# Row statistics of the first block-sparse layer made in attention's block, its bias and centroid operations apart from them, the weights' high parts on VectorE

## The reference

```python
x = x + attn_a(layernorm(x), w_attn, w_proj, adapter_wte, gating)   # 32 heads, rotary, adapter prefix
x = x + ffn(layernorm(x), weight, bias, centroids, assignments)     # first block-sparse layer
x = x + attn_b(layernorm(x), in_proj_w, conv_w, ..., out_w)         # state-space mixer, 128 heads
x = x + ffn(layernorm(x), weight, bias, centroids, assignments)     # the same layer again
...
def layernorm(x):
    m = mean(x, axis=-1); v = var(x, axis=-1)
    return (x - m) / sqrt(v + 1e-5)

def ffn(x, weight, bias, centroids, assignments):       # x: 1024 x 512, weight 512 x 512, 64 centroids
    dots = softmax(x @ centroids.T / 0.1, axis=-1)
    hits = dots > 0.01
    query_sel, cluster_sel = any(hits, axis=1), any(hits, axis=0)
    row_sel = cluster_sel[assignments]
    dense = x @ weight.T + bias
    return where(query_sel[:, None] & row_sel[None, :], dense, 0)
```

## Time and profile before

| | us |
|---|---|
| median of 3 runs | 1915.48 (1914.93 to 1915.66) |
| the profiled execution | 1914.4 |
| its span | 1912.7 |
| TensorE matmuls busy | 1817.4 (95%) |
| TensorE weight loads | 1454.2 (76%) |
| GpSimd | 1434.0 (75%) |
| VectorE | 1340.3 (70%) |
| ScalarE | 1163.2 (61%) |

### The profile page before, as it was taken

The page is one execution under the profiler, slowest core; times in us unless marked ns, Lnnn a source line. Parts: engine busy times, 40 slices in busy tenths (PEclk is TensorE's granted clock), DMA queues, the critical chain, the costliest instruction groups (busy, mean ns, idle before and its releaser), DMA issues.

```text
span 1912.7 us, 29241 instructions
## 1 busy us (share of the span) xinstructions
PE 1817.4 (95%) x10780; PEld 1454.2 (76%) x10780; DVE 1340.3 (70%) x1703; ACT 1163.2 (61%) x2105; POOL 1434.0 (75%) x1429
## 2 busy tenths in 40 slices
PE   6998897878999999999999999999999999999977
PEld 4776675667887888888888888888888888888866
DVE  5664564666767777687668767876777687678656
ACT  3222432358676777676676757766777577676752
POOL 4312333638997999799969978997899799979972
PEclk9997997989999999999999999999999999999999
DMA  3000001013222222222222222222322223213201
GB/s 111 1 2 23 2 1 59 12 55 104 90 83 83 78 94 100 67 90 88 89 78 78 94 72 86 94 91 70 96 78 94 72 89 99 95 62 115 72 23 44
DMA packets 107025, 135.54 MB, mean 71 GB/s; under 512 B 9026, under 2 KB 74690, under 8 KB 106884
## 3 DMA queue, kind: packets, MB, share of 16 engines
q1 hardware_dynamic: 105924, 133.63, 21.3%
q10 hardware_dynamic: 960, 0.05, 0.0%
HBM read 131.02 MB, written 2.62 MB: 70 GB/s over the span
## 4 chain that ended last, share of the span: by engine, by line
PE 78%; DVE 2%; POOL 1%; issue 1%; ACT 1%; DVEq 0%; POOLq 0%; ACTq 0%
PE ps L144 20%; PE ps L146 20%; PE ps L145 20%; PE ps L1928 7%; PE ps L1885 3%; PE ps L1929 3%; PE ps L1074 2%; PE ps L1913 1%; PE ps L1946 1%; PE ps L1948 0%; DVE mix_xT L1667 0%; DVE mix_u L1791 0%; PE ps L116 0%; POOL ffn_ln_mv L72 0%; DVE mix_xnT_lo L132 0%
## 5 line engine op out<-in xcount | busy, mean ns | idle before, releaser
L144 PE MATMUL ps<-mix_xnT_hi,mix_w_hi 128*128 128x512 f32 x1152 | 463.1, 402 | 9.5 <-DVE mix_bT L1667 9.5
L146 PE MATMUL ps<-mix_xnT_hi,mix_w_lo 128*128 128x512 f32 x1152 | 455.5, 395 | 0.0
L145 PE MATMUL ps<-mix_xnT_lo,mix_w_hi 128*128 128x512 f32 x1152 | 455.1, 395 | 0.0
L1667 DVE SCALAR_TENSOR_TENSOR mix_xT<-ps,mix_cur,mix_xT 128x510 f32<-128x510 f32 x378 | 279.2, 745 | 144.1 <-ACT mix_xT L1482 135.1
L1393 POOL TENSOR_SCALAR_AFFINE_SELECT mix_spread<-mix_spread 128x256 f32<-128x256 f32 x512 | 305.7, 631 | 0.0
L1687 DVE TENSOR_TENSOR mix_decay<-mix_decay,mix_cb 128x1536 f32<-128x1536 f32 x128 | 293.8, 2333 | 4.9 <-ACT mix_decay L1508 4.7
L1531 ACT ACTIVATE mix_g_hi<-mix_gated 128x512 fp32r<-128x512 f32 x128 | 81.0, 633 | 328.3 <-POOL mix_gated L1370 173.2
L144 PEld LDWEIGHTS ps<-mix_xnT_hi,mix_w_hi 128*128 128x128 f32 x1152 | 217.8, 189 | 58.4 <-issue 11.1
L146 PEld LDWEIGHTS ps<-mix_xnT_hi,mix_w_lo 128*128 128x128 f32 x1152 | 217.4, 189 | 50.9
L145 PEld LDWEIGHTS ps<-mix_xnT_lo,mix_w_hi 128*128 128x128 f32 x1152 | 217.9, 189 | 47.1
L1506 ACT ACTIVATE mix_decay<-mix_spread,mix_cur_ncum 128x256 f32<-128x256 f32 x512 | 253.7, 495 | 0.0
(11 more groups left out here) (262 smaller groups left out, 3327.0 us busy)
## 6 DMA issues: line engine op xcount, KB each, us to landing
mix_spread<-cum_rows SPq DMA_DIRECT2D x128, 512.0 KB, 4.0
mix_w_raw<-in_w_in_stream SPq DMA_DIRECT2D x144, 256.0 KB, 4.2
mix_wo_raw<-in_w_out_T SPq DMA_DIRECT2D x64, 256.0 KB, 3.6
att_w_raw<-in_w_attn_T SPq DMA_DIRECT2D x12, 256.0 KB, 4.1
x<-in_x SPq DMA_DIRECT2D x8, 256.0 KB, 4.4
out_rows<-x SPq DMA_DIRECT2D x8, 256.0 KB, 2.1
att_wp_raw<-in_w_proj_T SPq DMA_DIRECT2D x4, 256.0 KB, 2.6
mix_bT<-in_w_ffn_T SPq DMA_DIRECT2D x2, 512.0 KB, 4.9
```

Of the source, the lines that this page charges most:

```text
L144: pe.matmul(out, lh, rh, start=(k == 0), stop=False)
L145: pe.matmul(out, lh, rl, start=False, stop=False)
L146: last = pe.matmul(out, ll, rh, start=False, stop=(k == tiles - 1))
L1667: dve.scalar_tensor_tensor(out=d[:, :, shift:T], in0=src[:, :, 0:T - shift], scalar=w[:, MK - 1 - shift:MK - shift], in1=d[:, :, shift:T], ...
```

## The change

The statistics' two small tensors (`ffn_stats`, `ffn_mv`) are now allocated once for the whole program. In attention VectorE makes the statistics of row tiles 0 to 6 right after it has added the projection to x (`FFN_DONE` = 7), after a wait for that addition. GpSimd makes the scale and shift of these seven tiles behind its last mask, still in attention's block, on four semaphores of attention's own. In the layer only tile 7 is left: ScalarE waits for "shift" with tile 7 alone. GpSimd's list becomes `make`, the rows of tile 7, `split_bias` parts 0 and 1, `c_low`, `split_bias` part 2, `w_low`, `one_hot`. The centroids' high part moves on ScalarE from behind tile 1 to behind tile 2. The weights' four high parts leave ScalarE and stand on VectorE, behind the low parts of tiles 4, 5, 6 and 7. The last block-sparse layer keeps its order.

```diff
     def normalize_act(act, t):
-        act.wait_ge(ln.s["shift"], t + 1)
+        at_least(act, ln.s["shift"], t + 1 - done)
...
+            for t in range(FFN_DONE):
+                layernorm_rstd(pool, t, sh.ffn_mv, sh.mhalf, ffn_s, 0)
...
                 elif stage == "project":
                     dve.tensor_tensor(x[:, t, :], x[:, t, :], bank(n), ALU.add).then_inc(aux_free, 1)
+                    if t < FFN_DONE:
+                        dve.wait_ge(aux_free, n + 1)
+                        layernorm_stats(nc, dve, x, t, sh.ffn_stats, sh.ffn_mv, ffn_s, 0)
...
+FFN_DONE = NT - 1
...
+    def w_high_dve(dve, k):
+        dve.wait_ge(w_in, 32)
+        dve.tensor_copy(m.w_hi[:, k, :], m.w_raw[k // 2][:, k % 2, :]).then_inc(w_hi_done, 1)
...
             ln.hi_act(act, t)
-            if t == 1 and makes:
+            if t == 2 and makes:
                 act.wait_ge(c_in, 32)
                 act.copy(m.c_hi, m.c_raw).then_inc(c_done, 1)
-            if t >= NT - KT and makes:
-                w_high(act, t - NT + KT)
...
+    def first_rows_dve(dve):
+        for t in range(ln.done, NT):
+            ln.stats_dve(dve, t)
+        for t in range(NT):
+            ln.lo_dve(dve, t)
+            if t >= NT - KT:
+                w_high_dve(dve, t - NT + KT)
...
             f.make(pool)
-            for t in range(4):
+            for t in range(FFN_DONE, NT):
                 fln.rstd_pool(pool, t)
+            for part in range(2):
+                f.split_bias(pool, part)
             f.c_low(pool)
-            for part in range(3):
-                fln.rstd_pool(pool, 4 + part)
-                f.split_bias(pool, part)
-            fln.rstd_pool(pool, 7)
+            f.split_bias(pool, 2)
             for k in range(KT):
                 f.w_low(pool, k)
...
-            f.rows_dve(dve, lambda t: None)
+            f.first_rows_dve(dve)
```

More of the change, by code:

```diff
@@ L78, with build_layernorm @@
     pass
-def build_layernorm(nc, sh, ctx, tag, bank0, n=NT, into=None, banks=2, xn=None):
+def build_layernorm(nc, sh, ctx, tag, bank0, n=NT, into=None, banks=2, xn=None, kept=None, done=0):
     ln = Shared()
     ln.n = n
-    ln.stats = ctx.enter_context(nc.sbuf_tensor(tag + "_stats", [P, NT, 6], F32))
-    ln.mv = ctx.enter_context(nc.sbuf_tensor(tag + "_mv", [P, NT, 2], F32))
+    ln.stats, ln.mv = kept or (ctx.enter_context(nc.sbuf_tensor(tag + "_stats", [P, NT, 6], F32)),
+                               ctx.enter_context(nc.sbuf_tensor(tag + "_mv", [P, NT, 2], F32)))
+    ln.done = done
     ln.xn = xn
@@ L98, in stats_dve @@
     def stats_dve(dve, t):
-        layernorm_stats(nc, dve, sh.x, t, ln.stats, ln.mv, ln.s, 0)
+        layernorm_stats(nc, dve, sh.x, t, ln.stats, ln.mv, ln.s, -done)
     def rstd_pool(pool, t):
-        layernorm_rstd(pool, t, ln.mv, sh.mhalf, ln.s, 0)
+        layernorm_rstd(pool, t, ln.mv, sh.mhalf, ln.s, -done)
     def normalize_act(act, t):
-        act.wait_ge(ln.s["shift"], t + 1)
+        at_least(act, ln.s["shift"], t + 1 - done)
         at_least(act, ln.s["turned"], t - 1)
@@ L599, in build_attention @@
         y_inv, y_ready, y_hi_done = sem("y_inv"), sem("y_ready"), sem("y_hi_done")
+        ffn_s = {k: sem("ffn_" + k) for k in ("stat", "veps", "rstd", "shift")}
         block = ctx.enter_context(nc.Block())
@@ L1095, in layer_parts @@
     f.add_part, f.wait_x, f.rows_act, f.rows_dve, f.find_mask = add_part, wait_x, rows_act, rows_dve, find_mask
+    f.first_rows_dve = first_rows_dve
     f.take_dense, f.cluster_logits, f.turn_logits, f.dense_rows = take_dense, cluster_logits, turn_logits, dense_rows
@@ L1160, in build_mixer @@
         xn = square[:, :].rearrange("p (s c) -> p s c", c=C)
-        fln = build_layernorm(nc, sh, ctx, "ffn1_ln", 6, into=(xnT_hi, xnT_lo), xn=xn)
+        fln = build_layernorm(nc, sh, ctx, "ffn1_ln", 6, into=(xnT_hi, xnT_lo), xn=xn,
+                              kept=(sh.ffn_stats, sh.ffn_mv), done=FFN_DONE)
         chunks = lambda ap: ap.rearrange("p (k c) -> p k c", c=C)
@@ L2090, in build @@
         sh.mhalf = sb("minus_half", [P, 1])
+        sh.ffn_stats, sh.ffn_mv = sb("ffn_stats", [P, NT, 6]), sb("ffn_mv", [P, NT, 2])
         sh.x_arrived = [sh.sem(f"x_arrived{t}") for t in range(NT)]
```

## The result

The change takes 1907.94 us (median of 16 runs, 1901.62 to 1912.56) against 1915.04 us before (16 runs beside them, 1908.59 to 1916.23): ratio 0.9968, 95% interval 0.9959 to 0.9978. The prediction was 1913.5 us with "within 0.2%" at 0.81.

The account below looks back on a forecast made before the run. TensorE was 78% of the chain; the change acts where GpSimd's layer norm delays the cluster logits. 1.9 - 0.9 + 1.0 = 2.0 us earlier gave 1912.4 us, 1913.5 for the median, range 1911.0 to 1915.4.

Parts of the forecast that it names:

- GpSimd stood before the bias: First sparse layer: GpSimd waits 4.4 us for the bias transfer, taken to land at 329.5, holding up the centroids' low part.
- the first half: First 12 matmuls of the cluster logits: start at 333.8 instead of 335.70, 1.9 us earlier, mostly at low clock.
- tile 6 was turned: Transpose of tile 6 behind the logits' first half: 4.8 us after its start instead of 3.9, giving 0.9 back.
- from there to the second half: Tile 6's transpose to the logits' second half: 3.04 us instead of 4.06, gaining 1.0.
- Statistics in attention: Seven tiles' row statistics moved to VectorE in attention: cost on the path 0; 0.9 a tile if cover were gone.
- no weight was late: GpSimd's weight low parts end near 343.9, dense rows ask about 345.5: hidden by 1.5 us.
- A: Bias lands early or clock stays high in the logits' first half: gain 4.1 or 4.0, about 1911.4 us; chance 0.14.
- B: VectorE's copies collide with GpSimd at the shared port: gain only 0.4, time 1915.1 us; chance 0.13.
- C: Statistics lie on attention's path, delaying the yT copy: 3.2 us slower, 1918.7 us; chance 0.06.
- D: Barrier behind attention waits for GpSimd's tile 6, margin 0.5 us: gain 1.0, time 1914.5 us; chance 0.07.
- Nothing behind it has its own appointment: Behind the logits' second half: whatever comes earlier at its entrance stays earlier to the end, so the gain is 2.0 us.
- the sum's last line: Whole kernel: profiled 1914.4 - 2.0 = 1912.4 us, so 1913.5 for the median, from 1915.48 over three runs.

Follow-up runs that it names:

- the two kernels with a shorter first half: Change with centroids first, bias loaded earlier and unread matmuls in the layer (second: also in attention's last steps): 1903.21 us, 0.9960; 1906.20 us, 0.9968.
- the kernel with the new order alone: Kernel before with the change's GpSimd order, centroids' high part behind tile 2 and weight casts on VectorE, statistics still in the layer: 1914.85 us, one execution.
- the third: A further comparison of the unaltered change against the kernel before: ratio 0.9987, difference of means 2.1 us.
- The statistics alone: Change with only the statistics moved, GpSimd's old order kept (centroids first) and high parts back on ScalarE: 1907.53 us, ratio 0.9976 against before.

## Why the prediction failed

**What held.** GpSimd stood before the bias (4.4 us forecast, 4.95 measured, 4.4 to 5.1 in the four other executions). The centroids' low part stood behind it, the first half came 11.62 behind the start (11.38) and at the low clock, tile 6 was turned 4.26 us later (4.8; in the others 4.5 to 4.9), and from there to the second half it took 2.93 (3.04). The cast on VectorE was 0.42 alone (0.49). Statistics in attention cost nothing (1.0002), no weight was late. Each rival was thereby decided in its mechanism. A's does not hold: the bias is a brake, and the clock was low. B's collisions cost about 0.1 in the change, but 0.8 to 1.0 in the two kernels with a shorter first half. C did not occur, by the additions that moved by nothing. Nor did D, as GpSimd's first memset followed attention's end by 1.1 us before and now (322.42 - 321.3, 319.15 - 318.04).

On the landing of a small transfer, the Trainium skill (DMA: Bandwidth & Descriptors, "Queues, rings and completion order") says that completion is not in order of issue over one engine's transfers, but also that each DMA engine takes the descriptors of a ring in order. Here the order of issue decided: issued behind the weights the bias took 4.3 to 5.1 us in the executions of before and of the change, ahead of them 1.84. On the port, the Trainium skill (SBUF — State Buffer, "Who interferes with whom") says that casts from SBUF to SBUF can take the port pair that VectorE shares with GpSimd. The trace agrees: 0.98 and 1.46 us beside GpSimd, 0.42 alone.

**The step that failed** is in the first part: what the change is worth "is how much earlier than 343.65 that second half starts", with "Nothing behind it has its own appointment". TensorE's clock has one. Between the halves of the logits the kernel before left TensorE nearly idle, and in three of the five executions the clock then fell in the second half, which cost 1.6 us there. The sum had this term at nothing. (How far the idle time is the cause is shown in part only: matmuls in it removed the fall in two executions of two, but the kernel with the new order alone had the fall with the change's short wait.) The profile that I had shows an execution in which it did not, and gives 2.4 us for the layer; over five executions each, before has 26.3 us to the dense rows and the change 23.1, so **3.3 us**. The prediction had weighed the clock only in the first half.

**The second step** is the sum's last line. It took one profiled execution and three runs within 0.7 us as the kernel's own time. 16 runs of the same kernel spread over 7.6 us, 102 over 14. A forecast of 2.0 us from 1915.48 was thereby read against a median that lay 2.4 above the mean of all runs. Against that mean, 1913.1, the change's 1908.9 is a gain of 4.2 (2.9 to 5.5): the layer's 3.3 us lie within it, the 2.0 of the forecast do not. The first comparison alone, about 6 us, overstated it, and the third, 0.9987 (0.9970 to 1.0004), would have been called no change.

Together these make up the 5.6 us between the forecast of 1913.5 and the first comparison's 1907.94: 2.4 for the starting value, 1.3 for the layer, 0.9 of gain that nothing here explains, and 0.9 by which these 16 runs lay below the mean of the change's 42.

**Why a shorter layer isn't a shorter kernel to the same amount.** From the first dense row on, the same code took 1564.5 to 1569.3 us in the ten executions. Three stretches differ, each by 2.5 to 2.8 us: from the start of the eighth dense row to the mixer's first exponential of the decay 56.8 to 59.6 us, from there to the main loop's last product with the decay 1416.8 to 1419.3, and from that to the last layer's logits 35.1 to 37.6. The statistics alone gained 2.7 us on the change in the layer, and took 60.3 us for the first of these stretches, where the change mostly took 58.3. Whether the time at which a kernel gets there decides this was not tested; it is a matter of 2 us either way.

**What stays open:** the 0.9 us between 3.3 and 4.2, which is inside the interval. Attention's end: in the eleven profiles with the statistics in attention and nothing else added there it lies at 314.5 on average, in the eight without them at 316.5. Single ones lie from 311.8 to 321.3, so this is no clear difference, and the two executions alike to 0.02 us speak against one. And why the clock falls in before's second half in executions whose attention ends by 319.2 and not where it ends at 321.3, with TensorE as idle ahead of it, or in the kernel with the new order alone, which stands no longer than the change.

## What to carry to other kernels

Before a saving is measured from one profile, ask for a second execution of the same kernel, and see which stretches differ: here attention's end by 9.5 us, and the very layer by 1.6. Where TensorE stands nearly idle ahead of dense work, look in several executions whether its clock falls in that work, and count the slow matmuls as a possible part of the price: here 1.6 us in three executions of five. A collision that one order escapes can come back when something ahead of it gets faster, as the weight cast did (0.42 us, then 1.23 and 1.42). When a queue is reordered, look for the operation that waits for a transfer: what stands behind it inherits the wait (2.6 to 3.3 us here, for one line's place), and issuing that small transfer ahead of the large one cures it too.

## What was not expected of the hardware

- The granted clock of one kernel differs between executions by place: the same 12 matmuls take 2.8 us at 2.4 GHz and 5.1 at 1.2 in attention's last batch.
- A transfer of 4 KB landed 4.3 to 5.1 us after its issue behind 1 MB on the same queue, and 1.84 us after it ahead of that.
- A cast of 128x512 from SBUF on VectorE is 0.42 us alone and up to 1.46 beside GpSimd, while GpSimd's selects lengthen only from 0.61 to 0.68 and 0.80.
- Matmuls added to lift the clock cost time as long as it is still low: three took 1.49 us ahead of the transposes, and the first half of the logits began 1.2 to 1.5 us later than without them and took 1.3 to 1.7 us less.
